# Half of the attention transposes moved from TensorE to the DMA queue

## What is computed

```python
q = (q_lat @ q_b_w)...              # 32 heads: 128 plain and 64 rotary columns
kv = (rmsnorm(kv_lat, kv_a_norm_w) @ kv_b_w)...   # k_nope and v of 32 heads, from 64 latent columns
q_pe, k_pe = rope_interleaved(q_pe, pos), rope_interleaved(k_pe, pos)
scores = (q_nope @ k_nope.T + q_pe @ k_pe.T) * QKD ** (-0.5)
scores = jnp.where(mask[:, None], scores, -jnp.inf)   # mask = top 128 of the indexer, and causal
attn = jax.nn.softmax(scores, axis=-1)
out = jnp.einsum('bhqk,bhkd->bqhd', attn, v).reshape(b, s, H * VD)
return x + out @ o_w + experts(xn)
```

## Time and profile before

| | |
|---|---|
| median of the runs | 969.08 us (965.91 to 969.91) |
| the profiled execution | 972.53 us, its span 970.8 us |
| TensorE busy | 880.3 us, 91% of the span |
| VectorE busy | 740.9 us, 76% |
| ScalarE busy | 645.6 us, 67% |
| GpSimd busy | 367.4 us, 38% |
| DMA moved | 69.43 MB |
| mean granted clock of TensorE | 0.972 of 2.4 GHz |

### The profile page before, as it was taken

The page is one execution under the profiler, slowest core; times in us unless marked ns, Lnnn a source line. Parts: engine busy times, 40 slices in busy tenths (PEclk is TensorE's granted clock), DMA queues, the critical chain, the costliest instruction groups (busy, mean ns, idle before and its releaser), DMA issues. The chain is left out here.

```text
span 970.8 us, 21012 instructions
## 1 busy us (share of the span) xinstructions
PE 880.3 (91%) x7912; PEld 549.2 (57%) x7912; DVE 740.9 (76%) x1625; ACT 645.6 (67%) x1448; POOL 367.4 (38%) x291
## 2 busy tenths in 40 slices
PE   5979989968776989898889999999999999999998
PEld 2545544434443555555555777777777767774443
DVE  5366687899998999999998888888788888881100
ACT  3657799865674786777777777777777777880000
POOL 2093388754453544644554322322322323200000
PEclk9989999988886999999999999999999999999999
DMA  7012211112323145345443221111111111330111
GB/s 234 23 44 78 64 46 53 60 38 64 103 87 101 45 126 136 93 114 137 132 106 105 60 52 45 35 34 34 35 42 38 34 45 42 93 130 1 66 44 43
DMA packets 68259, 69.43 MB, mean 72 GB/s; under 512 B 8000, under 2 KB 50368, under 8 KB 68160
## 3 DMA queue, kind: packets, MB, share of 16 engines
q1 hardware_dynamic: 68160, 68.10, 25.4%
HBM read 36.62 MB, written 6.29 MB: 44 GB/s over the span
## 5 line engine op out<-in xcount | busy, mean ns | idle before, releaser
L712 ACT ACTIVATE arena<-psT 128x512 f16<-128x512 f32 (+4 forms) x516 | 242.8, 512 | 81.7 <-PE psT L666 71.4
L883 ACT ACTIVATE arena<-arena,small 128x512 f32<-128x512 f32 (+7 forms) x256 | 198.5, 775 | 65.0 <-DVE small L1131 64.4
L929 DVE SCALAR_TENSOR_TENSOR arena<-psT,arena 128x512 f16<-128x512 f32 (+3 forms) x392 | 206.2, 553 | 41.2 <-ACT arena L712 40.0
L621 PE MATMUL psS<-keyT,arena 128*128 128x512 f16 (+3 forms) x1152 | 231.7, 329 | 3.3 <-issue 3.3
L1131 DVE CUSTOM_DVE_ANT_0 arena<-psS,bias 128x512 f32<-128x512 f32 (+7 forms) x256 | 191.9, 750 | 37.4 <-PE psS L621 36.3
L666 PE MATMUL psT<-ident,arena 128*128 128x128 f32 x1152 | 177.4, 281 | 2.8 <-ACT arena L883 2.4
L621 PEld LDWEIGHTS psS<-keyT,arena 128*128 128x128 f16 x1152 | 102.9, 98 | 82.2 <-issue 25.8
L507 PE MATMUL psS<-ikT,big 128*128 128x512 f16 (+3 forms) x528 | 113.0, 362 | 30.7 <-DVE bias L1014 27.2
L640 PEld LDWEIGHTS psO<-val,arena 128*128 128x128 f16 x2976 | 109.6, 98 | 36.7 <-DVE arena L929 10.5
L666 PEld LDWEIGHTS psT<-ident,arena 128*128 128x128 f32 x1152 | 123.9, 141 | 4.9 <-ACT arena L883 2.3
L640 PE MATMUL psO<-val,arena 128*128 128x64 f16 x2976 | 118.3, 193 | 5.1 <-DVE arena L929 4.7
(11 more groups left out here) (150 smaller groups left out, 1147.9 us busy)
## 6 DMA issues: line engine op xcount, KB each, us to landing
arena<-arena SPq DMA_DIRECT2D x192, 128.0 KB, 2.4
arena<-in_wiq SPq DMA_DIRECT2D x32, 256.0 KB, 2.7
arena<-in_ow SPq DMA_DIRECT2D x16, 512.0 KB, 4.1
arena<-in_qbT SPq DMA_DIRECT2D x16, 256.0 KB, 2.5
wvo_parts<-arena SPq DMA_DIRECT2D x16, 256.0 KB, 2.7
arena<-in_qpe SPq DMA_DIRECT2D x16, 128.0 KB, 2.9
arena<-in_x SPq DMA_DIRECT2D x8, 256.0 KB, 2.9
out<-arena SPq DMA_DIRECT2D x8, 256.0 KB, 2.0
```

The source lines that it names most:

```text
L621: last = mm(bank[:, k:k + w], Q[:, u % 2, a, h, q:q + P], keyT[:, b, h, k:k + w], start=(a, b) == (0, 0), stop=(a, b) == (1, 0))
L712: return nc.scalar.activation(dst, src, ACT.Copy, scale=scale)
L883: nc.scalar.activation(pr[:, g % 4, 0:kw], pr[:, g % 4, 0:kw], ACT.Exp, bias=nmax[:, g % 4:g % 4 + 1], scale=-1.0, accum_out=rsum[:, unit_ ...
L929: return v.scalar_tensor_tensor(out=dst, in0=src, scalar=scale, in1=hi, op0=ALU.mult, op1=ALU.subtract)
```

## The change

Some steps no longer use TensorE for the transpose. `TURNED` lists them by their place in a unit: 1, 3, 5, 7 in pass one and 1, 3, 4, 5, 6, 7 in pass two. The two heads now alternate, so the odd places are the second head's tiles and, in pass two, 4 and 6 are the first head's tiles 6 and 5. In such a step VectorE adds log 1024 to the row shift (`nmax_s`), so that the exponential comes out scaled; ScalarE writes the high part as rows from `pr` to an fp16 row buffer (`rows_hi_`), GpSimd the low part (`rows_lo_`); SP issues one DMA transpose of both, 128 rows by 2 x (t + 1) blocks, to a column buffer (`turn`); `values` reads that buffer, four steps after the step instead of one (`LAG`). There are three row buffers and four column buffers, made from space that the double buffers of V and the indexer's arrays leave. The row sums of these steps are scaled too, which `unit_out` takes back by one more small product.

It also changes the order around this: the ring has three banks in pass one and two in pass two (the third is the output bank of every other unit); O and V change places; the copies and rope operations stand at fixed steps between the transposes; V has one buffer instead of two. Cut to its core:

```diff
+LAG = 4
+TURNED = ((1, 3, 5, 7), (1, 3, 4, 5, 6, 7))
         def tile_of(g):
-            return ORDERS[half_of(g)][g % 4]
+            return ORDERS[half_of(g)][g % 8 // 2]
+        def due(x):
+            return [g for g in (x - 1, x - LAG) if 0 <= g < STEPS and turns(g) == (g == x - LAG)]
 # SP
+            def turn(g):
+                d, nb = TURN_AT[g], tile_of(g) + 1
+                sp.wait_ge(row_lo, d + 1)
...
+                elif d >= 4:
+                    sp.wait_ge(av_mm, summed(BY_DMA[d - 4]))
+                sp.dma_start_transpose(cols_of_turn(d)[:, 0:2 * nb * P].rearrange("p (j q) -> p j q", q=P),
+                                       rows_of_turn(d)[:, 0:2 * nb * P]).then_inc(landed[d % 4], 16)
-            for u in range(NU - 2):
-                swap(u + 2)
-                place(u + 2, latent, qa_lo, q_lat, 1)
-                place(u + 2, turned, q_rot, q_tur, 0)
...
+            for g in range(STEPS):
+                u, s = divmod(g, 8)
+                if turns(g):
+                    turn(g)
+                if s == 1 and 2 <= u + 1 < NU:
+                    place(u + 1, latent, qa_lo, q_lat, 1)
+                if s == 2 and 2 <= u + 1 < NU:
+                    place(u + 1, turned, q_rot, q_tur, 0)
+                if s == 3 and u + 2 < NU:
+                    swap(u + 2)
...
 # TensorE
             for g in range(STEPS):
-                pe.wait_ge(exp_done, g + 1)
+                if not turns(g):
+                    pe.wait_ge(exp_done, g + 1)
...
-                if g:
-                    values(g - 1)
-            values(STEPS - 1)
+                for late in due(g):
+                    values(late)
...
-            for t in range(2):
-                products(t, t, range(NP))
-                experts(t, t)
+            products(0, 0, range(NP))
+            experts(0, 0)
+            for g in range(STEPS, STEPS + LAG):
+                for late in due(g):
+                    values(late)
+            products(1, 1, range(NP))
+            experts(1, 1)
 # ScalarE
+            def rows_hi_(g):
+                kw, d = P * (tile_of(g) + 1), TURN_AT[g]
+                if d >= 3:
+                    act.wait_ge(landed[(d - 3) % 4], landed_by(d - 3))
...
+                act.wait_ge(exp_done, g + 1)
+                copy(rows_of_turn(d)[:, 0:kw], pr[:, g % 4, 0:kw], 1.0).then_inc(row_hi, 1)
 # VectorE, row_max
-                if g >= 4:
+                if g >= 4 and turns(g - 4):
+                    dve.wait_ge(row_lo, TURN_AT[g - 4] + 1)
+                elif g >= 4:
                     dve.wait_ge(t_mm, TCUM[g - 3])
...
+                if turns(g):
+                    dve.wait_ge(max_done, g + 1)
+                    v.tensor_scalar(nmax_s[:, g % 4:g % 4 + 1], nmax[:, g % 4:g % 4 + 1], LOG_PR, None, ALU.add).then_inc(nmax_done, 1)
 # GpSimd
+            def rows_lo_(x):
+                kw, d = P * (tile_of(x) + 1), TURN_AT[x]
+                pool.wait_ge(row_hi, d + 1)
+                g.tensor_tensor(rows_of_turn(d)[:, kw:2 * kw], pr[:, x % 4, 0:kw], rows_of_turn(d)[:, 0:kw],
+                                ALU.subtract).then_inc(row_lo, 1)
+            for x in range(STEPS):
+                u, s = divmod(x, 8)
+                if x + 1 < STEPS and turns(x + 1):
+                    rows_lo_(x + 1)
+                if s == 0 and 2 <= u + 1 < NU:
+                    rope_low(u + 1)
+                if s == 3 and u + 2 < NU:
+                    rope_cos(u + 2)
+                if s == 5 and u + 2 < NU:
+                    rope_sin(u + 2)
...
```

More of the change, by code:

```diff
@@ L10 @@
+import math
 from contextlib import ExitStack
@@ L226, in block_kernel @@
         t_mm = sem("t_mm"); p_hi = sem("p_hi"); p_lo = sem("p_lo")
-        av_mm = sem("av_mm")
+        av_mm = sem("av_mm"); nmax_done = sem("nmax_done")
+        row_hi = sem("row_hi"); row_lo = sem("row_lo"); landed = [sem(f"landed{j}") for j in range(4)]
         ri_done = sem("ri_done"); o_done = sem("o_done")
@@ L252, in block_kernel, with summed, landed_by, rows_of_turn @@
             TCUM.append(TCUM[-1] + chunks(g_))
+        BY_DMA = [g_ for g_ in range(STEPS) if turns(g_)]
+        BY_PE = [g_ for g_ in range(STEPS) if not turns(g_)]
+        TURN_AT = {g_: d for d, g_ in enumerate(BY_DMA)}
+        FLIP_AT = {g_: d for d, g_ in enumerate(BY_PE)}
+        LOW_TURNS = NP * len(TURNED[0])
+        assert LOW_TURNS % 4 == 0 and 0 not in TURNED[0] and 0 not in TURNED[1]
+        def due(x):
+            return [g for g in (x - 1, x - LAG) if 0 <= g < STEPS and turns(g) == (g == x - LAG)]
+        AV_AT = {}
+        for x_ in range(STEPS + LAG):
+            for g_ in due(x_):
+                AV_AT[g_] = len(AV_AT)
+        def summed(g):
+            return AV_AT[g] + 1
+        UNIT_AV = [max(summed(g_) for g_ in range(8 * u_, 8 * u_ + 8)) for u_ in range(NU)]
+        def landed_by(d):
+            return 16 * (d // 4 + 1)
+        def rows_of_turn(d):
+            return rows_low[d % 3] if d < LOW_TURNS else rows_high[(d - LOW_TURNS) % 3]
+        def cols_of_turn(d):
+            return cols_low[d % 4] if d < LOW_TURNS else cols_high[(d - LOW_TURNS) % 4]
         RING = []
@@ L896, in ot_evac @@
                 copy(big[:, 0, p, c * CH:(c + 1) * CH], bank[:], O_S / (PR_S * K_S)).then_inc(ot_hi, 1)
-            exp_step(0)
-            exp_step(1)
+            for g in range(AHEAD - 1):
+                exp_step(g)
+                if turns(g):
+                    rows_hi_(g)
             for g in range(STEPS):
+                for use in uses_of(g):
+                    what, at, c = use
+                    if what == "T":
+                        p_hi_chunk(psT[BANK[use]], g, c)
+                if g + AHEAD - 1 < STEPS:
+                    exp_step(g + AHEAD - 1)
+                    if turns(g + AHEAD - 1):
+                        rows_hi_(g + AHEAD - 1)
                 for use in uses_of(g):
@@ L1214, in _ @@
             g.memset(eps_t, EPS).then_inc(eps_ok, 1)
+            for c in range(2):
+                cols = sorted(col_of(8 * NP * c + s) for s in TURNED[c])
+                g.memset(scaled[:, c, :], 1.0).then_inc(ones_ok, 1)
+                pool.wait_ge(ones_ok, c + 1)
+                for n, col in enumerate(cols):
+                    ins = g.memset(scaled[:, c, col:col + 1], PR_S)
+                ins.then_inc(eps_ok, 1)
             g.memset(bias[:], 0.0).then_inc(idx_init, 1)
@@ L1334, in _ @@
                     rope_low((8, 13).index(n))
-            for u in range(2, NU):
-                rope_turn(u)
-                q_low(u)
-                rope_low(u)
-                if u - 2 < NP:
-                    vo_low(u - 2)
+            for x in range(STEPS):
[8 more added lines that the diff above has]
+                    rope_sin(u + 2)
+                if s == 6 and u < NP:
+                    vo_low(u)
+                if s == 7 and u + 2 < NU:
+                    q_low(u + 2)
 def kernel(**inputs):
```

206 lines of the change are left out of this document (125 added, 81 removed).

## The result

The changed kernel takes 1051.15 us (median of four executions, 1049.68 to 1051.92) against 969.5 us for the kernel before on the same chip, a ratio of 1.0839 (95% interval 1.0793 to 1.0884). The forecast was 939 us with a range up to 1015: wrong in sign, and outside the range. The profiled execution's span is 1047.9 us, where it was 970.8. Counted in blocks, more than half of the transposes left TensorE: 10 of the 20 of a unit in pass one, 39 of the 52 in pass two.

A forecast was written before the change was run, and what follows sets the result against it. It took TensorE to bound pass two and mostly VectorE pass one. From the profiled 972.53 us, -33 - 1.2 - 16 + 20 gave 942.3, and 3.45 less for the median 939 us; own range 920 to 958, with rivals 908 to 1015.

The forecast's parts named there:

- I take 0.94, and 18.4 / 0.94 = 19.6 us: Pass two: ScalarE's 18.4 us of work, divided by an assumed busy share of 0.94, gives a 19.6 us unit, from 21.95.
- ScalarE, hidden until now, becomes the longest: Pass two: ScalarE at 18.4 us a unit would exceed TensorE's 17.5 and GpSimd's 17.3.
- Pass one: First pass over the heads: VectorE's 12.4 us over 0.955 gives 12.9 a unit, -16 us in all.
- 0, if the wait on landed data replaces it: Pass one's lower bound of gain: nothing saved if waiting for landed data takes over; the upper bound was 26 us.
- Loop: forecast -50: Both passes together: -33 us for 14 steady units of pass two, -1.2 for the last two, -16 for pass one.
- The tail: After the loop: folded-weight loads wait behind the last transpose, TensorE idle 17.1 us, then low clock 3 us; +20 us.
- prices of single operations: Costs assumed per new operation: copies near 1.05 us at 1024 columns, subtractions 2.1 to 2.4, small operations 0.2, issue 0.5.
- C: Rival, chance 0.27: DMA queue too slow for pass two, transposes under 138 GB/s or their issue holding SP; 1009 us.
- D: Rival, chance 0.03: DMA transposes go one transfer at a time, 25.5 us a unit in pass two; near 1080 us.
- B: Rival, chance 0.10: latency of three row buffers, each held through copy, subtraction, issue and landing; 21.5 us unit, 965 us.
- TensorE below 92%: Sign for the forecast in pass two: TensorE's busy share under 92% with ScalarE over 90% busy.
- the bound of 18.2: Pass two: shortest unit allowed, 18.2 us, with no losses and cheap copies.

The follow-up runs named there:

- e10_shift: Changed kernel with outputs evicted before the exponential, folded weights loaded early, L and O earlier in pass two, second head's tiles two places later: 967.99 us.
- e3_o_first: Changed kernel with ScalarE evicting the transposed output ahead of that step's exponential and row copy: 1001.82 us.
- e14_pass2_only: e11_one_input with DMA transposes in pass two only, none in pass one: 960.26 us.
- e11_one_input: e10_shift with VectorE's small product on the reciprocals made with one operand and a constant instead of two operands: 968.05 us.
- e12_five: e11_one_input with five steps instead of six by DMA in pass two, step 4 back on TensorE and L at step 5: 985.97 us.
- e15_early_sums: e14_pass2_only with the row sums' reciprocal and product at step 1 instead of 4, the output's product ahead of the row maximum, both passes: 947.13 us.
- e4_tail: Changed kernel with the folded weights loaded back in 16 transfers spread over pass two, not five behind the last transpose: 1037.28 us.
- e1_none: Changed kernel with no step transposed by DMA, all transposes on TensorE, new order and two-bank ring kept: 1077.81 us.

## Why the prediction was wrong

**The step that failed** is "I take 0.94, and 18.4 / 0.94 = 19.6 us", with "ScalarE, hidden until now, becomes the longest". It summed each engine's work and took the coupling, the share of its time in which the fullest engine is busy, from the old kernel, whose order had three banks, one step from exponential to values, and one exponential ahead of an output's eviction. The change's own description held what broke it: the ring of two banks in pass two, another place for the output's transpose, and both heads' exponentials and a row copy standing together on ScalarE. No term prices any of them. The unit came to 23.44 us, with ScalarE busy 188.54 of 260 us. The runs put 49 us on the eviction's place and leave 16 for L and O in the two-bank ring.

With both mended and the tiles shifted the unit is 20.21, near the 19.6 of the sum, but in part by luck. From the rows of e10_shift a unit holds 17.9 us of TensorE's work (230.11 / 260 x 20.21; forecast 17.5), 16.9 of ScalarE's (18.4), 16.4 of GpSimd's (17.3) and 13.8 of VectorE's (12.4). So ScalarE never became the longest; 1.1 us of its 18.4 were handovers, which are waiting and not work. And the fullest engine, TensorE, is busy 0.89 of the time, not 0.94.

**Pass one** was forecast at 12.9 and came to 15.64. The runs take it down in steps: 15.18 with the output evicted first (e3_o_first), 14.43 with no transposes by DMA in this pass (e14_pass2_only; e10_shift, e11_one_input and e12_five, which have them, show 14.92, 15.21 and 14.85), 13.56 with the sums early (e15_early_sums), which is still above 12.9. VectorE's work was forecast well, 12.4 us a unit against 146.60 / 180 x 15.64 = 12.7; what failed is again the coupling, 0.955 in the sum and 0.81 measured. The waits of TensorE's value products for VectorE's low evictions, 340 to 520 us, show where TensorE stood (before, then changed; us in total, times, longest):

```profile
PE psS L640 <- DVE arena L929: 6.2, 10, 1.4
PE psO L640 <- DVE arena L929: 4.1, 10, 1.0
```

```profile
PE psS L721 <- DVE arena L1038: 22.4, 15, 3.6
PE psO L721 <- DVE arena L1038: 18.4, 12, 2.9
```

Why the low evictions come late there is not settled beyond these steps. The bound "0, if the wait on landed data replaces it" ended on the wrong side: a loss was possible and left out.

**The accounting.** Loop: forecast -50, measured +57.6. The miss of 108 is 16 x (15.64 - 12.9) = 44 in pass one, 14 x (23.44 - 19.6) = 54 in pass two, and some 10 net between and around them: the three intervals between the two stretches took 64.5 us, where they had taken 50.9, the first reciprocal came 8.7 us later, and the last two units were shorter than before.

**The tail was right.** The forecast was that TensorE is idle for 17.1 us, released by a DMA, and then loses 3 us to a low clock, +20 in all. Measured is +19.5, in which the 78 value products behind the first output tile lie too.

```profile
930.35 0.60 PE L721 MATMUL psO<-val,arena 128*128 128x64 f16 x15
949.83 2.74 PE L766 MATMUL psS<-w1hi,big 128*128 128x512 f16 x6 [18.88 <-DMA sq<-wvo_parts]
```

The wait lasted 18.88 us, and the clock was 0.50 (1.2 of 2.4 GHz) in 949 to 953 and 0.98 in the next four. The six products took 2.74 us, where the twelve from 954.07 us on took 2.75, so the low clock cost less than 2 us, not 3. With the loads early (e4_tail) all but 0.4 of the 19.5 us are gone: 95.2 us follow the last reciprocal. The whole gains only 14, as the loop with the loads in it grew; its unit of pass two takes 23.77 us.

**Most prices of single operations were right.** One group of each new kind, by form, 560 to 900 us (busy, mean ns):

```profile
L1459 POOL TENSOR_TENSOR bias<-arena,bias 128x1024 f16<-128x1024 f32 x15 | 31.9, 2127 | 4.9 <-ACT bias L797 4.8
...
L797 ACT ACTIVATE bias<-arena 128x1024 f16<-128x1024 f32 x15 | 15.8, 1057 | 2.0 <-DMA arena<-bias 0.8
...
L1247 DVE TENSOR_SCALAR small<-small 128x1 f32<-128x1 f32 x85 | 13.1, 154 | 2.9
```

1.05 us a copy, 2.1 to 2.4 a subtraction and 0.2 an addition had been forecast. Landing was put at 3.8 us for 448 KB; the page of the profile gives 3.6 to 4.3 over all sizes (median us from issue to landing):

```profile
arena<-ikT SPq DMA_TRANSPOSE x75, 3.6
arena<-arena SPq DMA_TRANSPOSE x53, 3.8
arena<-bias SPq DMA_TRANSPOSE x32, 4.3
```

Two were wrong. The small product, put at 0.2 us, lasts 1.72, and the issue of a transpose, put at 0.5, lasts 1.4 to 2.0; the last section has their rows. No price of the sum covers a cast of VectorE (L1207) that grew from 0.42 to 1.84 us. In the changed kernel VectorE so has 174.96 / 260 x 23.44 = 15.8 us of work a unit, where 12.4 were forecast.

**The rivals.** C and D gave the right sign, and their times (1009, 1080) lie on both sides of the measured one, but by a mechanism that was not there: TensorE does not wait for landed transposes in the loop, and in e10_shift the same transposes fit into 20.21 us. B's wait exists, ScalarE on a row buffer, 15.0 us in eleven units, and half the bytes gained little of the loss. A slower outcome had a chance of 0.30, all of it on the DMA and none on TensorE's banks. Of the signs named, "TensorE below 92%" came true with ScalarE at 73%, which the text did not allow for. Two slips of the text changed nothing: the values come three steps later than before, not "two or four", and no term adds up to the bound of 18.2, as GpSimd's upper end is 18.0.

## What to carry to other kernels

When a change delays a consumer, count the buffers it keeps longer, and ask which ring gives them up: one PSUM bank of three, taken from the kernel before, cost 106 us by itself, where the transposes by DMA are worth 19 us in the best order found. Dividing summed engine work by an old coupling holds only for the old order; for a new order, follow one bank through its fill, both evictions and its next fill, and see what each engine does in between. An eviction that frees a bank for TensorE goes ahead of long work on its engine.

## What the runs showed of the hardware

**Some of VectorE's operations are held while GpSimd works.** The 128x8 product of two SBUF operands (L1260) has a mean of 1721 ns in pass two of the changed kernel and 167 in e1_none, where GpSimd has no row subtractions. VectorE, then GpSimd:

```profile
672.97 1.81 DVE L1260 TENSOR_TENSOR small<-small 128x8 f32<-128x8 f32 x1
```

```profile
672.87 1.88 POOL L1459 TENSOR_TENSOR bias<-arena,bias 128x896 f16<-128x896 f32 x1
```

It ends at 674.78, GpSimd's at 674.75. The cast at L1207, on 512 columns, has a mean of 1838 ns there and 416 in e1_none. The 128x1 operation with one operand (L1247, 154 ns) is not held, yet 128x6 with one operand is (964 ns in e11_one_input). The Trainium skill (SBUF — State Buffer, Who interferes with whom) says that VectorE with two SBUF inputs contends with GpSimd's reads, and that casts and tensor_scalar can take the shared port pair in their two-port modes; these rows agree. What it costs the kernel is not shown. Product and cast together are an estimated 3 us a unit more for VectorE (1.55 and 1.42), which is not full, and the one try to shorten the product left it at 964 ns.

**The rate of the DMA transposes.** Halving their bytes in the mended order, 1.28 of 2.56 MB a unit, lowered the DMA share from 0.95 to 0.59, so an estimated 0.36 x 20.2 = 7.3 us for 1.28 MB, some 175 GB/s. My 200 was near. The Trainium skill (Advanced Engine Details and Errata, X-Bar Transpose (TRN2)) gives 350-400 GB/s, twice what these transfers of 320 to 512 KB between two places in SBUF show. Half the bytes still took 2.6 to 3.1 us to land instead of 3.4 to 4.2 (medians by buffer).

**SP's issue of a transpose lasts** 1.42 to 1.96 us at the loop's end, where a load's lasts 0.51 to 1.05:

```profile
930.68 1.96 SPq L447 DMA_TRANSPOSE arena<-arena  x1
934.21 1.42 SPq L447 DMA_TRANSPOSE arena<-ikT  x1
...
936.63 0.52 SPq L471 DMA_DIRECT2D w1lo<-wvo_parts  x1
```

The forecast had 0.5 for it. Six of them are an estimated 10 us of SP's time a unit, and no wait of TensorE in the loop is put down to them.
